# Queries and keys in two rounded float32 parts, two heads in the two 64-row halves of TensorE, and a causal mask that TensorE adds before the row maxima

## The reference

```python
c_q = x @ W_dq;  Q = (c_q @ W_uq).reshape(Bx, Sx, N_HEADS, D_K)
c_kv = x @ W_dkv; K = (c_kv @ W_uk).reshape(...); V = (c_kv @ W_uv).reshape(...)
scores = jnp.einsum('bqhd,bkhd->bhqk', Q, K) / math.sqrt(D_K)
scores = jnp.where(causal, scores, -jnp.inf)
attn = jax.nn.softmax(scores, axis=-1)
out = jnp.einsum('bhqk,bkhd->bqhd', attn, V)
```

## Time and profile before

| | us |
|---|---|
| median of 3 runs | 1259.8 (1258.01 to 1261.18) |
| the profiled execution, span of its instructions | 1263.3 |
| attention's groups, first L1358 to the end of the last | 428.7 to 920 |

### The profile page before, as it was taken

How to read it: one execution, slowest core, us unless ns; L and a number is a source line. 1 busy time by engine, 2 the same in 40 slices (tenths; PEclk the granted TensorE clock), 3 DMA queues, 4 the chain that set the end, 5 groups by cost and what they waited for, 6 DMA issues and landing times. The chain is left out here.

```text
span 1263.3 us, 22520 instructions
## 1 busy us (share of the span) xinstructions
PE 1066.7 (84%) x6988; PEld 642.3 (51%) x6988; DVE 829.9 (66%) x2536; ACT 666.1 (53%) x1668; POOL 384.3 (30%) x404
## 2 busy tenths in 40 slices
PE   3539999984988899999999999999859369999940
PEld 2328888872442244443444444444347258888840
DVE  6774444436867888888888888888037754444427
ACT  5605554542753376676777666667636315455520
POOL 6506777752002000000000000000048227777730
PEclk8559999995977699999999999999889759999985
DMA  9503333326756444444444444440057113333339
GB/s 301 186 9 93 101 105 105 102 84 216 201 200 142 59 60 61 61 61 60 61 61 60 60 61 61 61 60 11 10 189 239 58 38 94 104 102 104 105 118 331
DMA packets 109248, 132.53 MB, mean 105 GB/s; under 512 B 29968, under 2 KB 83664, under 8 KB 109136
## 3 DMA queue, kind: packets, MB, share of 16 engines
q1 hardware_dynamic: 91280, 89.65, 31.2%
q0 software_dynamic: 13632, 37.24, 9.3%
q10 hardware_dynamic: 4224, 4.19, 1.0%
HBM read 82.42 MB, written 48.23 MB: 103 GB/s over the span
## 5 line engine op out<-in xcount | busy, mean ns | idle before, releaser
L1415 ACT ACTIVATE stacks_rows_or_prob<-stacks_bank 128x512 f32<-128x512 f32 (+3 forms) x768 | 326.0, 494 | 144.1 <-PE stacks_bank L1347 118.9
L1429 DVE CUSTOM_DVE_ANT_0 stacks_bank<-stacks_bank,all_causal 128x128 f32<-128x128 f32 (+3 forms) x512 | 245.4, 504 | 33.7 <-PE stacks_bank L1318 30.2
L1432 DVE TENSOR_REDUCE t_maxp<-stacks_bank 128x1 f32<-128x512 f32 x256 | 175.5, 686 | 25.0 <-PE stacks_bank L1318 24.4
L1318 PE MATMUL stacks_bank<-stacks_kst,stacks_qst 96*128 96x512 bf16 (+2 forms) x528 | 160.3, 348 | 8.5 <-DVE t_maxp L1429 4.2
L1358 PE MATMUL stacks_bank<-stacks_rows_or_prob,stacks_turned_or_values 128*32 128x512 f32 (+3 forms) x1536 | 164.5, 500 | 3.0 <-ACT stacks_rows_or_prob L1415 1.1
L1344 PE MATMUL stacks_bank<-stacks_qst,stacks_kst 99*128 99x512 bf16 (+3 forms) x528 | 154.9, 335 | 2.5 <-ACT stacks_rows_or_prob L1415 1.9
L1296 POOL COPY stacks_turned_or_values<-stacks_values 128x512 f32<-128x512 f32 x16 | 9.8, 613 | 427.7 <-DMA stacks_kst<-qk_parts 286.5
L1318 PEld LDWEIGHTS stacks_bank<-stacks_kst,stacks_qst 96*128 96x128 bf16 x528 | 48.5, 98 | 126.9 <-DVE t_maxp L1429 66.6
L653 PE MATMUL be_psG<-b_w,be_xT 128*128 x426 | 112.8, 401 | 0.0
L653 PE MATMUL ae_psG<-a_w,ae_xT 128*128 x426 | 111.9, 398 | 0.0
L1347 PE MATMUL stacks_bank<-all_causal_t,all_ident_bf 128*128 128x128 bf16 x512 | 109.6, 221 | 0.0
(11 more groups left out here) (296 smaller groups left out, 1917.7 us busy)
## 6 DMA issues: line engine op xcount, KB each, us to landing
stacks_qst<-qk_parts SPq DMA_DIRECT2D x66, 128.0 KB, 4.9
stacks_kst<-qk_parts SPq DMA_DIRECT2D x66, 128.0 KB, 7.6
stacks_rows_or_prob<-y_rows SPq DMA_DIRECT2D x16, 512.0 KB, 6.1
s_yk<-y_rows SPq DMA_DIRECT2D x16, 512.0 KB, 9.4
stacks_parts_or_stacks<-qk_parts SPq DMA_DIRECT2D x60, 128.0 KB, 6.2
qk_parts<-stacks_parts_or_stacks SPq DMA_DIRECT2D x16, 384.0 KB, 2.6
qk_parts<-q_parts SPq DMA_DIRECT2D x16, 384.0 KB, 3.4
o_rows<-t_orow SPq DMA_DIRECT2D x32, 136.0 KB, 8.7
```

The source lines that it names most:

```text
L1318: nc.tensor.matmul(psR[bank][:, 0:w], qst[slot][0:KROWS, h, i * P:(i + 1) * P], kst[slot][0:KROWS, h, k0:k0 + w], start=True, stop=True).t ...
L1415: nc.scalar.activation(prob[j % 2][:, h, a:(c + 1) * 512], psS[n % ST_BANKS][:, a - c * 512:512], ACT.Exp, scale=DK ** -0.5).then_inc(exp_ ...
L1429: ins = nc.vector.tensor_tensor_reduce(psR[bank][:, 0:w], psR[bank][:, 0:w], T.causal[:, 512 - w:512], 1.0, -BIG, ALU.add, ALU.max, maxp[: ...
L1432: ins = nc.vector.tensor_reduce(maxp[:, h, col:col + 1], psR[bank][:, 0:w], AX_X, ALU.max)
```

## The change

Queries and keys are split into two float32 parts rounded to the matmul's reduced float32 type (`F32R`) in place of three bfloat16 parts. ScalarE rounds the first, VectorE subtracts the second out; `take_high`, `middle` and their semaphores go. A stack has 3 blocks of 16 rows (48 rows, 50 with the two rows of the negated maximum) and lies twice on the partitions: even heads of the group on rows 0 to 63, odd heads on rows 64 to 127. Each score matmul so contracts over 48 or 50 rows in one half of the array, and it is at least 256 columns wide: the 128-column ones are widened. The bytes of a stack and of a load stay the same (12 loads of 128 KB a group); the parts stored for a unit grow from 384 to 512 KB; the rows of the maxima are written by 4 DMAs in place of 3. The ones below the key stack are set ahead of the loads, on 32 rows of each half, and SyncE waits for them.

In `score`, a unit that reaches the diagonal is followed by a matmul of the whole array that adds the mask to the bank, and `row_max` is a plain maximum for all units. `split_max` has two instructions in place of five. `score_units` puts the two heads of a pair next to each other, and `plan_step` has a clock for each half.

```diff
@@ -57,11 +57,14 @@
 EPS = 1e-5
 THRESHOLD = 0.7
 HALF = 0.5
-PARTS = 3
-Q_PARTS = (0, 0, 0, 1, 1, 2)
-K_PARTS = (0, 1, 2, 0, 1, 0)
+PARTS = 2
+Q_PARTS = (0, 0, 1)
+K_PARTS = (0, 1, 0)
 KROWS = len(Q_PARTS) * DK
 MROWS = KROWS + PARTS
+HALVES = 2
+HALF_ROWS = P // HALVES
+ROUNDED_COLS = 256
...
-        last = [self.parts_or_stacks[:, i * (HG * S // 2):(i + 1) * (HG * S // 2)].bitcast(BF16).rearrange("p (h t) -> p h t", h=HG)
+        last = [self.parts_or_stacks[:, i * (HG * S // 2):(i + 1) * (HG * S // 2)].bitcast(F32R).rearrange("p (c t) -> p c t", c=self.PAIRS)
                 for i in range(2)]
-        self.qst = [M.sb(f"qst{s}", [P, HG, S], BF16) for s in range(SLOTS - 1)] + [last[0]]
-        self.kst = [M.sb(f"kst{s}", [P, HG, S], BF16) for s in range(SLOTS - 1)] + [last[1]]
+        self.qst = [M.sb(f"qst{s}", [P, self.PAIRS, S], F32R) for s in range(SLOTS - 1)] + [last[0]]
...
         self.loaded = [M.sem(f"loaded{s}") for s in range(SLOTS)]
+
+    def rows(self, st, slot, h, n):
+
+        at = (h % HALVES) * HALF_ROWS
+        return st[slot][at:at + n, h // HALVES, :]
 
     def load(self, sp, g, slot):
...
             for r, part in enumerate(which):
                 src = self.qk_dram[kind, part, bass.ds(hg * (HG * DK), HG * DK), bass.ds(b * S, S)]
-                sp.dma_start(st[slot][r * DK:(r + 1) * DK, :, :],
-                             src.rearrange("(h d) t -> d h t", d=DK)).then_inc(self.loaded[slot], 16)
+                by_half = src.rearrange("(c a d) t -> a d c t", a=HALVES, d=DK)
+                for a in range(HALVES):
+                    at = a * HALF_ROWS + r * DK
+                    sp.dma_start(st[slot][at:at + DK, :, :].bitcast(F32), by_half[a]).then_inc(self.loaded[slot], 16)
 
 
 def programs_qkv(nc, ctx, T, tag, R, x, y_dram, A, Q):
...
+                sp.wait_ge(Q.ones_ready, HALVES * (SLOTS - 1))
                 stacks(0)
...
             def low(u):
-                dve.wait_ge(mid_ready, c * NU + u + 1)
-                nc.vector.tensor_tensor(parts[b][:, u, 2, :], bank(c, u)[:], parts[b][:, u, 1, :], ALU.subtract).then_inc(low_ready, 1)
+                dve.wait_ge(high_ready, c * NU + u + 1)
+                nc.vector.tensor_tensor(parts[b][:, u, 1, :], bank(c, u)[:], parts[b][:, u, 0, :], ALU.subtract).then_inc(low_ready, 1)
...
-        def take_high(c, b, u):
-            pe.wait_ge(high_ready, c * NU + u + 1)
-            nc.tensor.matmul(bank(c, u)[:], T.minus_bf[:], parts[b][:, u, 0, :], start=False, stop=True,
-                             skip_group_check=True).then_inc(high_taken, 1)
...
             up(c, b, 0)
             up(c, b, 1)
             values(c, b, 0)
-            take_high(c, b, 0)
+            up(c, b, 2)
             if more:
                 turn(c + 1, 1 - b)
-            take_high(c, b, 1)
-            up(c, b, 2)
             up(c, b, 3)
-            take_high(c, b, 2)
             Q.early_scores(pe, c, 1)
             if more:
                 latents(c + 1, 1 - b)
-            take_high(c, b, 3)
             values(c, b, 1)
             Q.early_scores(pe, c, 3)
...
                 high(c, b, 0)
                 high(c, b, 1)
-                middle(c, b, 0)
                 copy_values(c, b, 0)
-                middle(c, b, 1)
+                high(c, b, 2)
                 if more:
                     copy_turned(c + 1)
-                high(c, b, 2)
                 high(c, b, 3)
-                middle(c, b, 2)
                 if ahead:
                     ln.deviation(act, c + 2)
                 if more:
                     copy_latents(c + 1, 1 - b)
-                middle(c, b, 3)
                 copy_values(c, b, 1)
...
 def score_units():
 
     units = []
-    for h in range(HG):
+    for pair in range(HG // HALVES):
         for i in range(QT):
             end = (i + 1) * P
-            units.append((h, i, 0, min(end, 512), i))
-            if end > 512:
-                units.append((h, i, 512, end - 512, i + QT // 2))
+            for k0 in range(0, end, 512):
+                for a in range(HALVES):
+                    units.append((pair * HALVES + a, i, k0, min(end - k0, 512), i + k0 * QT // (2 * 512)))
     return units
...
         start, _, what = min(can)
         if what == "r":
             kind, u = ring[n_ring][:2]
             w = units[u][3] if kind == "s" else 512
-            t = start + w / 2.4
-            dve = max(dve, t + READER_LATENCY) + 64 + (w if kind == "s" else 900) * 1.04
+            end = start + max(w, ROUNDED_COLS) / 2.4
+            if kind == "s":
+                half_free[units[u][0] % HALVES] = end
+                t = start + ISSUE
+                if units[u][2] + w == (units[u][1] + 1) * P:
+                    end = t = max(half_free) + P / 2.4
+                    half_free = [end] * HALVES
+            else:
+                half_free = [end] * HALVES
...
         def load_max(g, slot):
-            wait(sp, m_ready, g + 1)
-            for part in range(PARTS):
-                sp.dma_start(qst[slot][KROWS + part:KROWS + part + 1, :, :], mparts[:, part, :]).then_inc(m_loaded, 16)
+            wait(sp, drained, max_at(g))
+            for a in range(HALVES):
+                at = a * HALF_ROWS + KROWS
+                rows = slice(a * (MROW // HALVES), (a + 1) * (MROW // HALVES))
+                for part in range(PARTS):
+                    sp.dma_start(qst[slot][at + part:at + part + 1, :, :].bitcast(F32),
+                                 mparts[rows, part, :].bitcast(F32)).then_inc(m_loaded, 16)
...
+        sp.wait_ge(Q.ones_ready, HALVES * SLOTS)
         A.load(sp, 2, 2)
...
+    def ones(pool, s):
+
+        for a in range(HALVES):
+            rows = slice(a * HALF_ROWS + HALF_ROWS // 2, (a + 1) * HALF_ROWS)
+            Q.ones_chain.link(nc.gpsimd.memset(kst[s][rows, :, :].bitcast(F32), 1.0))
...
     def score(pe, u, slot, r, bank):
         h, i, k0, w, _ = units[u]
         wait(pe, drained, r + 1 - RING_BANKS)
-        nc.tensor.matmul(psR[bank][:, 0:w], qst[slot][0:KROWS, h, i * P:(i + 1) * P],
-                         kst[slot][0:KROWS, h, k0:k0 + w], start=True, stop=True).then_inc(filled, 1)
+        wide = max(w, ROUNDED_COLS)
+        diagonal = k0 + w == (i + 1) * P
+        ins = nc.tensor.matmul(psR[bank][:, 0:wide], A.rows(qst, slot, h, KROWS)[:, i * P:(i + 1) * P],
+                               A.rows(kst, slot, h, KROWS)[:, k0:k0 + wide], start=True, stop=not diagonal)
+        if diagonal:
+            ins = nc.tensor.matmul(psR[bank][:, w - P:w], T.causal_t[:], T.ident_bf[:], start=False, stop=True)
+        ins.then_inc(filled, 1)
...
         def score_t(g, k, j, c, h):
             n, a = n_st[j, c, h], max(c * 512, j * P)
             ps = psS[n % ST_BANKS][:, a - c * 512:512]
+            wide = min(a, (c + 1) * 512 - ROUNDED_COLS)
             wait(pe, exp_done, g * ST + n + 1 - ST_BANKS)
-            ins = nc.tensor.matmul(ps, kst[k][0:MROWS, h, j * P:(j + 1) * P], qst[k][0:MROWS, h, a:(c + 1) * 512],
-                                   start=True, stop=a > j * P)
+            ins = nc.tensor.matmul(psS[n % ST_BANKS][:, wide - c * 512:512], A.rows(kst, k, h, MROWS)[:, j * P:(j + 1) * P],
+                                   A.rows(qst, k, h, MROWS)[:, wide:(c + 1) * 512], start=True, stop=a > j * P)
             if a == j * P:
                 ins = nc.tensor.matmul(ps[:, 0:P], T.ident_bf[:], T.causal_t[:], start=False, stop=True)
             ins.then_inc(st_done, 1)
...
     def row_max(dve, u, r, bank):
 
         h, i, k0, w, col = units[u]
+        half, pair = h % HALVES, h // HALVES
         dve.wait_ge(filled, r + 1)
-        if k0 + w == (i + 1) * P:
-            ins = nc.vector.tensor_tensor_reduce(psR[bank][:, 0:w], psR[bank][:, 0:w], T.causal[:, 512 - w:512], 1.0, -BIG,
-                                                 ALU.add, ALU.max, maxp[:, h, col:col + 1])
-        else:
-            ins = nc.vector.tensor_reduce(maxp[:, h, col:col + 1], psR[bank][:, 0:w], AX_X, ALU.max)
-        ins.then_inc(drained, 1)
+        nc.vector.tensor_reduce(maxp[:, half, pair, col:col + 1], psR[bank][:, 0:w], AX_X, ALU.max).then_inc(drained, 1)
...
         def split_max(g, r, bank):
 
             dve.wait_ge(filled, r + 1)
-            wait(dve, m_loaded, g * (16 * PARTS))
-            nc.vector.tensor_scalar(neg[:], psR[bank][0:MROW, 0:P], -1.0, None, ALU.mult).then_inc(drained, 1)
-            dve.wait_ge(drained, r + 1)
-            link(nc.vector.tensor_copy(mparts[:, 0], neg[:]), g, 2)
-            link(nc.vector.tensor_tensor(mid[:], neg[:], mparts[:, 0], ALU.subtract), g, 3)
-            link(nc.vector.tensor_copy(mparts[:, 1], mid[:]), g, 4)
-            nc.vector.tensor_tensor(mparts[:, 2], mid[:], mparts[:, 1], ALU.subtract).then_inc(m_ready, 1)
+            wait(dve, m_loaded, g * M_LOADS)
+            turned = psR[bank][0:MROW, 0:P]
+            link(nc.vector.tensor_scalar(mparts[:, 0], turned, -1.0, None, ALU.mult), g, 2)
```

(2 more changed lines are left out.)

93 lines of the change are left out of this document (52 added, 41 removed).

## The result

The changed kernel takes **2008.01 us** (median of 4 runs, 2006.32 to 2010.30), the kernel before beside it 1258.9 us (4 runs, 1254.86 to 1261.18): a ratio of **1.597, 95% interval 1.590 to 1.604**. The prediction was 2047 us. The profiled execution has a span of 2006.8 us, against 1263.3 before.

What follows compares the result with a forecast made beforehand. TensorE was taken to bound the kernel. Fourteen groups x 51.7 = 724 us, +43 and +28 for the last two, -8 outside: +787 on 1263.3, 2050, less 3.5 for the median: 2047 us; range 1530 to 2130.

Steps and rivals of the forecast that it cites:

- the likeliest case: Whole kernel: costly entries and exits, with 1.2 GHz for most of attention; 1930 to 2130 us, chance 0.62.
- Price of going in and out: TensorE, common group: 68 entries, 65 exits and 12 entries into `pv` cost 29.6 us at 1.2 GHz, 22.7 at 2.4.
- Columns and waits: TensorE, common group at 1.2 GHz: streams 49.8 us, issue 1.3, small waits between engines 1.7.
- The last groups: Last two attention groups: 76.0 us against 33.20 and 53.2 against 24.70, adding 43 and 28 us.
- The clock: Attention: an emptier array brings 1.2 GHz for most of it; a group takes 82.4 us, 50.6 at 2.4 GHz.
- VectorE: Common group: plain maxima at the diagonal save 5.0 us of VectorE's time, worth nothing since TensorE bounds the group.
- Ahead of attention: Projections -5 us (-20 to +15) and units before group 0 -3 us (-6 to +10), together -8.
- Rival B: Attention: the clock holds at 2.4 GHz, so the kernel takes 1552 us; chance 0.16.
- C: Entries into halves: weight loads hide while the whole array works; 43.3 us a group, near 1440 us; chance 0.05.
- D: Scores: the halves never overlap, 6.6 us more a group at 1.2 GHz, 2140 us; chance 0.03 with anything beyond 2130.
- E: Attention: masks and 48-row matmuls pass without emptying the array and heads pair up; faster, 1166 us; chance 0.04.

Runs made afterwards that it cites:

- run 8: Changed kernel with both parts as bfloat16 in the same halves, masks still over the whole array (leaves out the second part's precision): 1743.4 us.
- run 9: Kernel before, with only the whole-array mask of the transposed scores made two 64-row matmuls of 64 columns: 1331.3 us.
- run 1: Changed kernel with each mask made two matmuls of 64 columns over 64 rows, in its scores' half: 1310.2 us.
- run 2: As run 1, and the planner no longer lets both halves meet at a mask: 1315.5 us, ratio 1.043.
- run 4: Changed kernel with a whole-array mask held back where the next score is in the other half, so two masks come together: 1689.7 us.
- run 3: Changed kernel with only the masks of the scores for the maxima put into halves, those of the transposed scores whole-array: 1730.7 us.
- run 5: Kernel before, with only the diagonal score mask moved to TensorE and plain maxima on VectorE: 1271.8 us, ratio 1.013.
- run 10: Kernel before, with TensorE's mask and plain maxima for the first group's score units only: 1252.9 us, ratio 0.9985.
- run 11: Changed kernel with both masks left out, so causality is missing from the result: 1311.0 us.
- run 12: As run 11, with VectorE's maxima over at most 192 columns and a smaller scale in the exponential: 1244.8 us.
- run 6: Changed kernel with the maxima's mask back on VectorE and the transposed scores' mask in the head's own half: 1333.3 us, ratio 1.058.
- run 7: As run 6, with score matmuls of 128 columns not widened to 256: 1344.6 us.

## Why the prediction was right, step by step

**Forecast and range.** Slower by far, 2047 us against 2008, and the likeliest case is the one that came. Between the two profiled spans 787 us were foretold and 743.5 measured: 33 of the surplus are in the fourteen common groups (724 against 691) and 12 in the last two, with 1.6 the other way outside the groups.

**Price of going in and out.** "68 x 0.30 + 65 x 0.11" at 1.2 GHz is in sum what the rows show to 0.01 us. How it was split between going in and out is not: the starts have 0.10 to 0.11 ahead of the half-array score and 0.30 behind it. With 68 and 65 of them the sum hardly depends on that. The cause was tried from three sides: take the changes away and keep everything else (runs 1 and 2), take the four-byte load away and keep the changes (run 8, 12.4 us), add changes where nothing else differs (run 9, 0.10 each way at 2.4 GHz). That a part of it is a load that does not hide was right too: 0.19 of the 0.41 by run 8 is the four-byte load's, and the rest is as long as two-byte loads.

**Columns and waits.** The 1.7 us of small waits, kept in the sum, are not there. TensorE's whole idle time in the common group of the trace is one wait:

```profile
PE stacks_bank L1396 <- ACT stacks_rows_or_prob L1452: 0.4, 1, 0.4
```

Those 1.3 us are most of 82.4 - 80.3. Without waits 80.7 us were foretold and 79.9 measured, so columns, issue and changes hold as a sum; the columns by themselves were not measured.

**The last groups** were mis-sized: 76.0 and 53.2 foretold, 70.9 and 45.8 measured. The prediction gives their sums without the counts, so which term was too large can't be said for sure. In the trace they go 56 and 31 times into the halves, where a common group goes 68 times.

**The clock** was the riskiest step and held: 0.50 through all of attention, from 379 on. Its share is not seen in the changed kernel itself, which had no group at 2.4 GHz. By run 4's ratio of 1.66 such a group would take 80.3 / 1.66 = 48 us (an estimate; 50.6 foretold), so of the 49.6 us more a group about 18 belong to the order of shapes and about 32 to the clock. The two come together: run 1 takes most of the changes away and gets nearly all of both back. The reason given for the fall, an emptier array, is not shown. Kernels with 96 rows kept 2.4 GHz with 25 changes a group and with 82 (before, run 9), one with 48 rows and 29 changes kept it through twelve of sixteen groups (run 1), and one with 48 rows and 84 changes had it seldom (run 3): neither the rows nor the changes alone brought the low clock for most of attention here. Rival B, that the clock holds, is out. The Trainium skill ("TensorE: Matmul & The Clock Gate", "Why this matters for your kernels") ties the fall to idle gaps. The traces don't bear that out as the only way down: in run 4 the clock fell with TensorE busy 10.00 of the 10.00 us before, although the short losses around the changes count as busy there.

**VectorE** "5.0 us less a group, worth nothing": worth nothing, yes, but the size was wrong. The 141 ns rows of the accumulator's read the earlier trace rows lie mostly beside the instructions around them, and summing mean durations counted them as time. Run 5 has 1.0 us.

**Ahead of attention**, -8 foretold and -5.8 in the two traces. This can't be called confirmed: the start of group 0 lies 14 us apart in the traces of before and of run 10, two kernels whose totals can't be told apart, and single totals of before run from 1247 to 1264 us in one set of runs.

**Rivals.** C: the load doesn't hide. D: pairs at one start (817.57) refute it. E needed both free changes and full overlap; runs 11 and 12 show that even with no mask at all a group takes 31.3 and 30.3 us, hardly less than the 30.7 of before. The Trainium skill ("TensorEngine Tiling (Array Packing)", "Theoretical Speedup") gives up to twice the speed for contractions over at most 64 rows; in these traces pairs came near it, of 512 and of 256 columns, and no group as a whole did. The same page says under "Key Properties" that a change of tiling mode drains the array. Every entry and exit shows a loss; that it is a drain, and not a load left unhidden, the rows don't tell.

## What to carry to other kernels

Count how often a kernel's order changes the array's shape before halving the height of a matmul: here 145 changes a group cost more than the halves could save, and one small whole-array matmul between two halves was enough to make most of them. Give a helper matmul (a mask, a bias) the tile shape of its neighbours, even as two pieces. And price a change at both clock levels, since halves with many changes between them went with the lower one here, and by the estimate above it cost more than the changes themselves.

## What the runs showed of the hardware

- A change between whole array and 64-row halves costs 0.10 us each way at 2.4 GHz (run 9) and 0.11 at 1.2 GHz when the weights are two-byte (run 8); a four-byte 128-column weight adds 0.19 at 1.2 GHz. Each loss is as long as the weight load of the matmul it stands behind (291, 103 and 105 ns in the changed kernel and run 8).
- A TensorE that the profile calls over 99% busy can stay at 1.2 GHz for 1124 us of groups, and the clock can fall behind 10.00 busy us of 10.00 (run 4). In that busy time the short losses around changes are counted. Kernels whose scores have 96 to 99 rows kept 2.4 GHz through nearly all common groups, with 25 changes a group and with 82 (before, runs 5, 9, 10). With 48 to 50 rows some kept it (run 12), some lost it now and then (runs 1, 2, 6, 7, 11), all with about 30 changes a group, and those with 84 to 145 had it seldom or never (the change, runs 3, 4, 8).
- One and the same group takes 64.8 us at the one level and 39.0 at the other (run 4): 1.66, not 2. What a change costs hardly grows at the lower clock (0.10 and 0.11), which goes with that.
- Matmuls with four-byte weights in different halves can start together, those of 512 columns (the changed kernel, 817.57) and those of 256 (run 12, 510.99). A group without any mask still takes 30.3 to 31.3 us against 30.7 before (runs 12 and 11).
